# Scatters of the routed tokens in every step, and expert work from an earlier quad

## The reference

```python
h = dAt * h + dBt * xt[..., None]
h_norm = jnp.sqrt(jnp.sum(h * h, axis=(1, 2), keepdims=True))
scale = jnp.minimum(20.0 / (h_norm + 1e-08), 1.0)
h = h * scale
y = jnp.einsum('bdn,bn->bd', h, Ct) + Dp * xt
```

## Time and profile before

| | us |
|---|---|
| median of 3 runs | 1629.64 (1629.27 to 1631.2) |
| profiled execution, its own time | 1625.1 |
| its span in the trace | 1623.4 |
| DVE busy | 1527.7 (94%) |
| TensorE busy | 1274.5 (79%) |
| ScalarE busy | 1160.8 (72%) |
| GpSimd busy | 772.5 (48%) |

### The profile page before, as it was taken

How to read it: one execution, slowest core, us unless ns; L and a number is a source line. 1 busy time by engine, 2 the same in 40 slices (tenths; PEclk the granted TensorE clock), 3 DMA queues, 4 the chain that set the end, 5 groups by cost and what they waited for, 6 DMA issues and landing times.

```text
span 1623.4 us, 34377 instructions
## 1 busy us (share of the span) xinstructions
PE 1274.5 (79%) x9628; PEld 1117.0 (69%) x9628; DVE 1527.7 (94%) x9635; ACT 1160.8 (72%) x2944; POOL 772.5 (48%) x1254
## 2 busy tenths in 40 slices
PE   5665536589899888989989898899989798835661
PEld 4554435478788777878878787788878687734550
DVE  6889888999999999999999999999999999987798
ACT  7887647477787868877787877778787777846550
POOL 4267766444444444444444444344444444478852
PEclk9767667799999999999999999999999999968795
DMA  9921111200111020120012012111201100012255
GB/s 342 323 71 52 43 41 44 99 18 24 42 57 43 16 76 24 37 74 24 24 42 69 18 30 68 37 31 35 65 16 42 58 24 16 20 41 74 70 164 184
DMA packets 85088, 104.56 MB, mean 64 GB/s; under 512 B 7712, under 2 KB 75936, under 8 KB 84896
## 3 DMA queue, kind: packets, MB, share of 16 engines
q1 hardware_dynamic: 76848, 85.47, 16.2%
q0 software_dynamic: 6144, 16.79, 3.2%
q10 hardware_dynamic: 1904, 0.09, 0.1%
HBM read 56.45 MB, written 45.88 MB: 63 GB/s over the span
## 4 chain that ended last, share of the span: by engine, by line
DVE 33%; PE 31%; POOL 15%; ACT 12%; issue 7%; DMA 2%; POOLq 0%; ACTq 0%; SPq 0%; DVEq 0%
PE ps L1258 10%; PE ps L1242 8%; POOL arena L520 7%; DVE arena L728 6%; DVE arena L706 6%; PE ps L1230 5%; DVE arena L722 5%; DVE arena L714 5%; DVE arena L700 4%; POOL xg L503 4%; DVE arena L684 3%; ACT arena L872 3%; PE ps L1224 3%; POOL wf L509 2%; POOL wp L509 2%
## 5 line engine op out<-in xcount | busy, mean ns | idle before, releaser
L520 POOL TENSOR_TENSOR arena<-arena,neghalf 128x1 f32<-128x1 f32 x1025 | 601.8, 587 | 782.1 <-DVE arena L703 734.3
L728 DVE SCALAR_TENSOR_TENSOR arena<-arena 128x128 f32<-128x128 f32 x1024 | 361.6, 353 | 23.4 <-POOL arena L520 23.4
L1230 PE MATMUL ps<-arena,pick 128*128 128x128 f32 x2048 | 303.6, 296 | 63.3 <-ACT arena L989 40.2
L1230 PEld LDWEIGHTS ps<-arena,pick 128*128 128x128 f32 x2048 | 279.7, 211 | 77.9 <-ACT arena L989 65.3
L1242 PE MATMUL ps<-arena,wf 128*128 128x256 f32 x1280 | 305.9, 390 | 19.6 <-issue 8.1
L989 ACT ACTIVATE arena<-ps,arena 128x128 f32<-128x128 f32 x1024 | 292.4, 375 | 30.8 <-PE ps L1230 29.0
L1258 PE MATMUL ps<-wp,arena 128*128 128x256 f32 x1280 | 295.1, 384 | 9.1 <-ACT arena L1004 6.0
L706 DVE CUSTOM_DVE_ANT_0 arena<-arena 128x128 f32<-128x128 f32 x1024 | 299.1, 292 | 2.2
L714 DVE CUSTOM_DVE_ANT_0 arena<-arena 128x128 f32<-128x128 f32 x1024 | 293.3, 286 | 2.8 <-ACT arena L989 2.1
L700 DVE TENSOR_TENSOR arena<-arena 128x128 f32<-128x128 f32 x1024 | 291.7, 285 | 0.0
L1242 PEld LDWEIGHTS ps<-arena,wf 128*128 128x128 f32 x1280 | 242.7, 196 | 52.2 <-issue 9.2
(11 more groups left out here) (149 smaller groups left out, 1331.2 us busy)
## 6 DMA issues: line engine op xcount, KB each, us to landing
xg<-zeros SPq DMA_DIRECT2D x10, 1024.0 KB, 10.7
xrow<-xg SPq DMA_DIRECT2D x40, 256.0 KB, 2.8
yg<-arena SPq DMA_DIRECT2D x40, 256.0 KB, 2.2
arena<-in_x SPq DMA_DIRECT2D x16, 512.0 KB, 9.3
wf<-in_c_fc SPq DMA_DIRECT2D x8, 1024.0 KB, 5.1
wp<-in_c_proj SPq DMA_DIRECT2D x8, 1024.0 KB, 6.0
ys<-arena SPq DMA_DIRECT2D x66, 64.0 KB, 1.6
xnd<-arena SPq DMA_DIRECT2D x8, 512.0 KB, 6.4
```

The source lines that it names most:

```text
L520: g.tensor_tensor(sv[:, slot, 1:2], mx, neghalf[:, 0:1], ALU.pow).then_inc(s_ready, 1)
L728: v.scalar_tensor_tensor(hr[:, slot, :], vv, sv[:, before, 1:2], ur[:, slot, :], ALU.mult, ALU.add)\
L1230: last = t.matmul(ps[2][:, j * P:(j + 1) * P], pick[:, q * QUAD + j, :], xin, start=True, stop=True)
```

## The change

The 64 scatters stand in steps 16 to 79, one in each, in place of every second step from 16 to 142. Expert work is laid over quads 25 to 229 (205 quads) in place of 41 to 229 (189). The wait ahead of each scatter, the number of scatters and their sizes, the fetches and the end of the expert work stay. With the table of steps the order of DVE's instructions in those steps (`sending`) and the steps of its input pieces (`delayed`) move too, and with the planner's quads the blocks at which SP loads weights and rows.

```diff
-        QUADS, MOE_AT, MOE_QUADS, COMBINE_AT, LAST_HALF = NT // QUAD, 41, 230, 237, 240
+        QUADS, MOE_AT, MOE_QUADS, COMBINE_AT, LAST_HALF = NT // QUAD, 25, 230, 237, 240
...
         SEND_AT, FETCH_AT = 16, 930
-        at_step = {SEND_AT + 2 * n: ("send", n) for n in range(2 * TILES)}
+        at_step = {SEND_AT + n: ("send", n) for n in range(2 * TILES)}
         at_step.update({FETCH_AT + n: ("fetch", n) for n in range(2 * TILES)})
```

## The result

The changed kernel takes 1689.26 us (median of 3, 1688.62 to 1689.45) against 1629.64: a ratio of 1.0362, 95% interval 1.0339 to 1.0386, so 59.6 us more. The forecast was 1687, with a range of 1681 to 1696. The profiled execution took 1689.26, its span 1687.5, which is 64.1 more than the span of before: the trace of before is of an execution 4.5 us under its median, that of after is of one at its median.

A forecast was written before the change was run, and what follows sets the result against it. The recurrence on DVE, waiting for POOL's power, was taken to set the end step by step. Scatters +59.5 and the stall -2.4 gave +57: 1682 on the profiled 1625.1, 1687 us with the median's 4.5; range 1681 to 1696.

The forecast's parts named there:

- The interval of 2.76: Scatter steps 16 to 79: issues 2.76 us apart, from landing 2.5 plus 0.25 to 0.3 to the next issue; bounds 2.70, 2.80.
- The handing on: POOL's queue: the next step's power stands behind the waiting scatter, DVE's scan and update behind that, so each step takes 2.76.
- Late landings: Scatter steps: lateness on top of the 2.76 intervals, 4.7 us with 0.3 for scatters at block starts.
- the halving of the lateness: Scatter steps: 4.5 us of lateness tied to the instruction stream becomes 2.3, as that moves by half as many steps.
- The stall of 2.4: Block of 16 steps around 1014 us: expert work from quad 25 removes 2.4 us; bounds -2.4 and +2.2.
- scatters paced by POOL's loop: Rival, scatter steps: POOL's loop, not the landing, sets 1.87 a step; 1625.5 us, faster by 0.25%; 3 in 100.
- shortened with DVE idle: Rival, scatter steps: scatters land sooner when DVE stands idle; a landing 0.2 shorter gives 1674 us; 3 in 100.
- lengthened by packing: Rival, scatter steps: landings get later when packed; each second one 1 us late gives +32, 1719 us; 4 in 100.
- The estimate of 2.30: Skill's rule for a 128 KB scatter, 2.0 us plus bytes over 436 GB/s: interval 2.55 to 2.60, whole change near +47.
- the exclusion of DVE and POOL: Skill's shared pair of ports, a possible mechanism for landings shortening with DVE idle; the scatter at 90.86 does not show it.

The follow-up runs named there:

- Two in flight: The changed kernel with two semaphores in turn, each scatter waiting for the landing of the one before the last: 1628.65 us, 0.9998 of before.
- The pair without the power: Two kernels without POOL's power (state's scale always 1), expert work from quad 49: scatters in every step 1694.33 us, in every second step 1622.97 us.
- expert work at quad 41: The changed kernel with expert work back at quad 41 in place of 25, scatters still in every step: 1690.19 us, 1.0381 of before.
- expert work alone: The kernel before with expert work from quad 37 in place of 41, scatters still in every second step: 1641.0 us, 1.0068 of before.
- one-pair kernel: The kernel before with its last scatter moved from step 142 to 141, so two scatters stand in consecutive steps once: 1631.17 us, one execution.
- second trace of before: The kernel before, unchanged, traced again: 1625.19 us.
- both kernels with two in flight in every second step: The kernel before with two scatters in flight: 1627.7 us, 0.998 of before; the same with expert work from quad 37: 1636.35 us, 1.0033.

## Why the prediction was right, and where it was not

- **The time came nearer than the change did.** From trace to trace the kernel lost 64.1 us, where the forecast had +57.1; by the medians it lost 59.6. I had carried the 4.5 us between the trace of before and its median over to the changed kernel, as if its executions would show it too. They do not: the traced one is at the median of three that lie within 0.9 us. So 4.5 of the 7.0 us of error came back by luck; without it the time would have been 1693.8, still inside the range. Why executions of before differ by up to 13 us (1624.11 to 1637.22) no run here shows.
- **The interval of 2.76** held: 2.75 on the chip. Two in flight took it away, and the loss with it. That it is built from one late landing in the trace of before was the useful step: the wait that would bind was already there, four times.
- **The handing on** held for this kernel: power behind scatter, scan and update behind power. The pair without the power shows that the reason is wider than I had it: whatever POOL does for the others stands behind the scatters, and 64 x 2.75 us of POOL's queue have to fit into the steps they are given. In 128 steps they do, in 64 they don't.
- **Late landings** were mis-sized. I took 4.7 us. Measured: the last scatter issues at 264.69, the first at 83.14; less 63 x 2.755 = 173.6 that leaves 8.0. The step that failed is the halving of the lateness with the number of steps. Landing by landing, six of 64 were over 0.2 us late before, 7.5 in all, and eight after, 7.6 in all. The instruction packets did become fewer while the scatters ran (7 of 16 KB and 16 of 8 KB before, 4 and 9 after); the lateness did not.
- **The stall of 2.4** went, so the term came out, but its reason did not hold: it also went with expert work at quad 41. With expert work alone, from quad 37, that block takes 23.18 too, but shorter waits of DVE stand elsewhere. What removes it is not settled. It is 24.84 - 23.24 = 1.6 us in the one-pair kernel, 26.32 - 23.17 = 3.2 in the second trace of before, so its size moves from trace to trace of nearly the same kernel.
- **A term was missing**: plain steps 0.3% longer, 720.47 - 718.30 = 2.2 us in 496 steps and 395.09 - 393.82 = 1.3 in the next 272. It takes back what the stall gave: from step 144 on the kernel loses 1.1 where I had -2.4.
- **What bounds a plain step** was read too simply. I said that DVE waits for POOL's power only at scatters and fetches, from the named waits. They name none in a plain step, and yet the power binds it: in a plain step of after L728 starts at 600.47, 0.04 behind the end of the power that starts at 599.85 and takes 0.58, and without the power the step is 0.05 shorter. The number did not depend on it.
- **The rivals**: scatters paced by POOL's loop is what two in flight made, 1.83 to 1.92; with the wait kept it could not be. Landings neither shortened with DVE idle nor lengthened by packing: median 2.5 in every kernel with the power. While the scatters ran, DVE waited 74.8 of 182.4 us for POOL (under half, not over half as I had said), and a scatter took 1.04 on POOL and 2.5 to land, as before. The estimate of 2.30 for such a transfer by the Trainium skill (DMA: Bandwidth & Descriptors, anatomy of a DMA from POOL) does not show here. Nor does the exclusion of DVE and POOL that the Trainium skill states for some of DVE's operations (SBUF — State Buffer, two separate sides).

## What to carry to other kernels

A wait that costs nothing because something lies between is a price tag: add the landing and the handover, and that is the interval as soon as the space in between goes. Before packing transfers closer, give them a second semaphore so that two may be in flight; here that was worth 60 us at one spacing and 2 (by the medians) to 4 (by the traces) at the other. And look at everything that stands behind a waiting instruction in its queue, to the next thing that another engine needs, not to the nearest alone; what starts when the transfers are done has to keep its distance too.

## What the runs showed of the hardware that was not expected

- Scatters in consecutive steps, and one pair of them is enough, make POOL's power about 5 ns longer for the rest of the recurrence. Eleven traces here have the power. Ahead of the first scatter its mean is 580 to 582 ns in all of them. Between 500 and 900 us it is 580 in the five without consecutive scatters (before twice, expert work alone, both kernels with two in flight in every second step) and 584 to 585 in the six with them. It goes with the kernel and not with how long an execution took: that of expert work alone took 1637.97 us and has 580. By L728, 496 plain steps take 717.7 to 718.3 us with the shorter power and 720.2 to 720.5 with the longer, where no other wait stands in them. The power lies on the path of the step, so it shows in the time: 768 x 5 ns is 3.8 us, beside the 2.2 + 1.3 above. What in POOL changes is open.
- Without the power between them, scatters came 3.13 apart (229.36 to 232.49) although they landed in 2.4: the handover from a landing to the next issue took about 0.7, against 0.25 to 0.3 where POOL worked in between. The same trace has both: with L527 between two scatters they stand 2.67 apart (235.62 to 238.29). The expectation of 2.76 was wrong there, and the cause is open.
